# A graph network on one core: source rows of the first stage gathered during the dense pass and kept in a table in DRAM

## What is computed

```
def _gin_conv(x, src, dst, wa, ba, wb, bb):
    agg = segment_sum(x[src], dst, num_segments=N_NODES)
    h = x + agg
    h = relu(h @ wa + ba)
    return h @ wb + bb
```

## Time and profile before

| | |
|---|---|
| median of 3 runs | 4950.94 us (4936.32 to 4970.49) |
| the profiled execution, by its own time | 4992.41 us |
| its span, first to last instruction | 4990.6 us |
| mean granted TensorE clock | 0.735 of full |
| POOL busy | 1923.9 us (39%), 1994 instructions |
| PE busy | 3052.7 us (61%) |

### The profile page before, as it was taken

The page is one execution under the profiler, slowest core; times in us unless marked ns, Lnnn a source line. Parts: engine busy times, 40 slices in busy tenths (PEclk is TensorE's granted clock), DMA queues, the critical chain, the costliest instruction groups (busy, mean ns, idle before and its releaser), DMA issues. The chain is left out here.

```text
span 4990.6 us, 67455 instructions
## 1 busy us (share of the span) xinstructions
PE 3052.7 (61%) x18081; PEld 2462.8 (49%) x18081; DVE 2653.8 (53%) x8166; ACT 2245.8 (45%) x5893; POOL 1923.9 (39%) x1994
## 2 busy tenths in 40 slices
PE   1182019997887787785663059991089891068665
PEld 1062007775443454443563049890089891067664
DVE  2092009998343655896562017770047881078875
ACT  0082008885111344674552027770056770066765
POOL 6606750000554554663664720007700007700455
PEclk8596559998776878997786569885588875576655
DMA  3292016665554343454663237672256762255443
GB/s 115 68 341 101 12 38 221 221 224 171 139 153 118 95 108 109 135 170 136 185 202 106 63 114 232 203 220 65 59 182 203 221 198 80 65 173 193 137 130 93
DMA packets 419338, 723.50 MB, mean 145 GB/s; under 512 B 76431, under 2 KB 137908, under 8 KB 418606
## 3 DMA queue, kind: packets, MB, share of 16 engines
q1 hardware_dynamic: 350990, 610.53, 37.8%
q0 software_dynamic: 63040, 107.35, 8.6%
q10 hardware_dynamic: 5024, 2.30, 0.2%
HBM read 428.65 MB, written 321.10 MB: 150 GB/s over the span
## 5 line engine op out<-in xcount | busy, mean ns | idle before, releaser
L683 POOL DMA_INDIRECT msgs<-t_gat,row_i x591 | 567.1, 960 | 1180.2 <-DMA t_gat<-t_hn 951.1
L1738 PE MATMUL t_p_q<-mean_col,t_nsq 128*128 128x1 f32 x2352 | 344.5, 268 | 285.7 <-issue 228.5
L1738 PEld LDWEIGHTS t_p_q<-mean_col,t_nsq 128*128 128x128 f32 x2352 | 354.5, 231 | 297.3 <-issue 297.3
L2246 ACT ACTIVATE t_nnt<-t_p_nt,cxt 128x512 f32<-128x512 f32 x294 | 200.6, 682 | 614.3 <-remote 235.6
L699 POOL DMA_INDIRECT dg_g_ring<-t_xw,src_i x197 | 189.6, 962 | 669.1 <-DVE slot_id L1202 603.6
L2083 PE MATMUL t_p_nt<-ident,t_nh 128*128 128x128 f32 x1176 | 222.6, 322 | 252.2 <-issue 181.0
L1731 PE MATMUL t_p_nh<-wx,t_nnt 128*128 128x132 f32 x1568 | 261.0, 317 | 188.0 <-issue 138.6
L2006 POOL DMA_INDIRECT out_rows<-t_hn,own_i x197 | 200.5, 1018 | 416.8 <-issue 336.6
L1731 PEld LDWEIGHTS t_p_nh<-wx,t_nnt 128*128 128x128 f32 x1568 | 224.7, 218 | 189.0 <-issue 188.9
L2083 PEld LDWEIGHTS t_p_nt<-ident,t_nh 128*128 128x128 f32 x1176 | 163.2, 166 | 267.9 <-issue 252.5
L1752 DVE TENSOR_TENSOR t_hn<-t_p_nh,t_ninv 128x264 f32<-128x264 f32 x392 | 151.4, 428 | 257.8 <-remote 194.2
(11 more groups left out here) (410 smaller groups left out, 8730.8 us busy)
## 6 DMA issues: line engine op xcount, KB each, us to landing
t_gat<-t_hn SPq DMA_DIRECT2D x296, 264.0 KB
t_nh<-t_gat SPq DMA_DIRECT2D x294, 264.0 KB
t_x<-de_x SPq DMA_DIRECT2D x196, 256.0 KB
t_ah<-t_gat SPq DMA_DIRECT2D x150, 264.0 KB
t_gat<-de_h SPq DMA_DIRECT2D x98, 264.0 KB
t_xw<-in_x_map SPq DMA_DIRECT2D x28, 903.0 KB
de_xt<-in_x_t SPq DMA_DIRECT2D x98, 256.0 KB
t_xn<-t_x SPq DMA_DIRECT2D x98, 256.0 KB
```

Source lines behind the costliest of these rows:

```text
L683: self.nc.gpsimd.indirect_dma_start(out=self.msgs[:, c, 0:width], out_offset=None, in_=table, in_offset=bass.IndirectOffsetOnAxis(ap=idx[: ...
L1738: last = self.nc.tensor.matmul(p_q[:, j:j + 1], sq[:, j * D:(j + 1) * D], self.mean_col[:], start=True, stop=True)
L2246: nc.scalar.activation(nnt[:, g % 2], p_nt[:], ACT.Identity, bias=bias).then_inc(act_nt, 1)
```

## The change

POOL no longer fills the ring for gin1 directly. During the dense pass it gathers each group of source rows into the same ring, waits until the group before has landed, and writes that group with a plain DMA of its own to a new table in DRAM, `t_xs` (128 x 200 x 129 numbers). The place in the ring is free again when the write of four groups earlier has landed (`kept`). In gin1 SP loads each group from the table into a new tile `xs` of four groups, ahead of the flags; it waits for the group's write, and for PE and DVE to have left the tile's place. PE and DVE wait for this load where they waited for the gathers. SP's steps of gin1 are written out, where they were a loop.

```
-        def rows(i):
-            u = i % UN
-            if i >= UN:
-                pool.wait_ge(turned, i - UN + 1)
-                pool.wait_ge(taken, i - UN + 1)
-            for j in self.filled(i):
-                nc.gpsimd.indirect_dma_start(
-                    out=ring[:, u, j, :], out_offset=None, in_=self.xw,
-                    in_offset=bass.IndirectOffsetOnAxis(ap=self.src_i[:, i * G4 + j:i * G4 + j + 1], axis=0)).then_inc(arrived[u], 16)
...
-        for i in range(AG):
-            rows(i)
+        for i in range(AG + 1):
+            if i < AG:
+                u, c0 = i % UN, i * G4
+                if i >= UN:
+                    pool.wait_ge(kept[u], 16 * (i // UN))
+                for j in self.filled(i):
+                    nc.gpsimd.indirect_dma_start(
+                        out=ring[:, u, j, :], out_offset=None, in_=self.xw,
+                        in_offset=bass.IndirectOffsetOnAxis(ap=self.src_i[:, c0 + j:c0 + j + 1], axis=0)).then_inc(arrived[u], 16)
+            if i > 0:
+                u, c0, n = (i - 1) % UN, (i - 1) * G4, len(self.filled(i - 1))
+                pool.wait_ge(arrived[u], self.ring_rows((i - 1) // UN + 1, i - 1))
+                nc.gpsimd.dma_start(self.xs[:, c0:c0 + n, :], ring[:, u, 0:n, :]).then_inc(kept[u], 16)
...
+            xs = sb("xs", [128, UN, G4, MW])
+            arrived = [sem(f"arrived{u}") for u in range(UN)]
...
                     if live(k, u, 0, AG):
+                        c0, n = i * G4, len(self.filled(i))
+                        sp.wait_ge(kept[u], 16 * (i // UN + 1))
+                        wait(sp, s["pe_t"], i - UN + 1)
+                        wait(sp, s["dve_row"], i - UN + 1)
+                        sp.dma_start(xs[:, u, 0:n, :], self.xs[:, c0:c0 + n, :]).then_inc(arrived[u], 16)
                         wait(sp, s["dve_s"], i - UN + 1)
...
-                steps(sp, AG, 6, step, 2)
+                written_out(AG, 6, step)
...
-                        pe.wait_ge(arrived[v], self.ring_rows(k + (0 if u < 1 else 1), i - 1))
+                        pe.wait_ge(arrived[v], 16 * (k + (0 if u < 1 else 1)))
```

More of the change, by code:

```diff
@@ L245, in allocate @@
         self.xw = xw[0:NPAD * MW].rearrange("(r w) -> r w", w=MW)
+        self.xs = nc.dram_tensor("t_xs", (128, CHUNKS, MW), F32, kind="Internal").ap()
         self.unplaced = xw[NPAD * MW:NPAD * MW + SLOTS].rearrange("(p c) -> p c", p=128)
@@ L685, in resident_gather, with slot_gathers @@
                 in_offset=bass.IndirectOffsetOnAxis(ap=idx[:, c:c + 1], axis=0), **bound).then_inc(arrived, 16)
-    def slot_gathers(self, pool, ring, sem, arrived, turned, taken):
+    def slot_gathers(self, pool, ring, sem, arrived, kept):
         nc, a = self.nc, self.a
         mapped = sem("g_mapped")
-        def rows(i):
-            u = i % UN
-            if i >= UN:
-                pool.wait_ge(turned, i - UN + 1)
-                pool.wait_ge(taken, i - UN + 1)
-            for j in self.filled(i):
-                nc.gpsimd.indirect_dma_start(
-                    out=ring[:, u, j, :], out_offset=None, in_=self.xw,
-                    in_offset=bass.IndirectOffsetOnAxis(ap=self.src_i[:, i * G4 + j:i * G4 + j + 1], axis=0)).then_inc(arrived[u], 16)
         self.resident_gather(self.dst_i, a["x"], D, self.got, range(FIRST, FIRST + EVERY * COPIES))
@@ L1048, in hidden, with gin1_part @@
         return t[:, bass.ds(g, 1), 0:GN].rearrange("p o f -> p (o f)")
-    def gin1_part(self, block, sem, xs, arrived, turned, taken):
+    def gin1_part(self, block, sem, kept):
         nc, a = self.nc, self.a
@@ L1065, in gin1_part @@
             names = ("pe_x", "pe_r", "pe_a", "pe_b", "pe_h", "dve_b", "act_a", "act_b", "dve_s", "dve_r", "dve_e",
-                     "dve_h", "least", "mix", "blank_rows")
+                     "dve_h", "least", "mix", "blank_rows", "pe_t", "dve_row")
             s = {n: sem(n) for n in names}
-            s["pe_t"], s["dve_row"] = turned, taken
             own = lambda c: self.msgs[:, bass.ds(c, 1), 0:D].rearrange("p o f -> p (o f)")
@@ L1200, in step @@
                     if live(k, u, 1, AG):
-                        dve.wait_ge(arrived[v], self.ring_rows(k + (0 if u < 1 else 1), i - 1))
+                        dve.wait_ge(arrived[v], 16 * (k + (0 if u < 1 else 1)))
                         nc.vector.tensor_copy(self.slot_id[:, bass.ds((i - 1) * G4, G4)], xs[:, v, :, D]).then_inc(s["dve_row"], 1)
@@ L1231, in phase_dense_gin1 @@
             arrived = [sem(f"g_arrived{u}") for u in range(UN)]
-            turned, taken = sem("g1_turned"), sem("g1_taken")
-            self.dense_part(block, lambda n: sem("de_" + n), lambda pool: self.slot_gathers(pool, ring, sem, arrived, turned, taken))
-            self.gin1_part(block, lambda n: sem("g1_" + n), ring, arrived, turned, taken)
+            kept = [sem(f"g_kept{u}") for u in range(UN)]
+            self.dense_part(block, lambda n: sem("de_" + n), lambda pool: self.slot_gathers(pool, ring, sem, arrived, kept))
+            self.gin1_part(block, lambda n: sem("g1_" + n), kept)
     def phase_gin2(self):
```

## The result

| | before | changed |
|---|---|---|
| median of 4 runs each | 4954.82 us (4936.32 to 4970.49) | 5054.97 us (5050.42 to 5075.88) |
| ratio of the two | | 1.0209, 95% interval 1.0178 to 1.0240 |
| span of the profiled execution | 4990.6 us | 5057.6 us |
| first scan of gin1 | 1233.8 us | 1459.4 us, +225.6 |
| first to last scan | 337.4 us | 221.3 us, -116.1 |

The change costs 100 us, 2.1%. Its sign, its place and its two opposite parts are as predicted. The loss in the dense pass is 48 us smaller than predicted.

What follows compares the result with a forecast made beforehand. The prediction took the phase up to gin1 as bound by POOL's issuing and PE, one after the other. Dense pass +274 and gin1 -112 gave +162 us, 4950.9 + 162 = 5113 us, range 4980 to 5190.

Steps and rivals of the forecast that it cites:

- its two opposite parts: Dense pass loses 274 us under POOL's added issuing; gin1 without POOL gains 112 us; together +162 us.
- The main step: Dense pass: POOL's unbroken issuing lasts 289 us longer, delaying PE's signals; gin1 then runs at 4.54 us a step.
- Rival A: Dense pass: lag doesn't follow the gathers, which stay hidden; only gin1's gain is left, 4839 us; chance 0.09.
- The rule quoted from the Trainium skill: Engines: only DVE and GpSimd share a port, PE and ACT never wait; by it the 274 us would be nearly nothing.
- the 62 predicted for the writes: POOL in the dense pass: 50 table writes, each priced at a gather's 1.25 us, 62 us in all.
- The new waits: POOL in the dense pass: waits for `arrived` and `kept` should be met when reached, costing nothing.
- The dense pass: Under 289 us more issuing at 123.2 us a group, 2.3 groups worth 15 us get done: loss 274 us.
- the 26 us of tail: Dense pass: lag outlasting POOL's last gather, 718.4 to 744.6 us, expected alike before and after the change.
- rival B: Dense pass: new waits open pauses letting others catch up; 4986 us; 0.15 including what lies between it and the forecast.
- C: POOL's writes are dear, 2.1 us each or more: 5156 us, or 5212 with late gin1 loads; 0.10 beyond the forecast's range.
- gin1: All 49 steps at 4.54 instead of 6.89 us: 115 us less, taken as 112 for the first steps' clock.
- the likeliest case: Whole kernel: forecast of 5113 us with its own range, 5060 to 5160 us, chance 0.66.

Runs made afterwards that it cites:

- paced kernels: Kernel before with POOL's dense-pass DMAs in bursts of five gathers or four scatters: 4576.39 us; changed kernel in bursts of five at most: ratios 0.992 and 0.9241.

## Why the prediction was right, and where it was off

**The main step held.** The gathers moved into the dense pass lengthen the time in which PE's signals come late; gin1 then has its undisturbed pace. Rival A, that they are hidden, gave 4839 us; the kernels with plain loads or no gathers came to 4836 and 4852 us, so its sum was near and only its condition wasn't met where the lag is. The rule quoted from the Trainium skill (page "SBUF — State Buffer", section "Who interferes with whom") can't be carried over to ACT's waits at semaphores: with the lag they were 44 to 48 us. On the chip without it the traces agree with the rule: PE does 1028 matmuls beside 120 DMAs of POOL.

**POOL's issuing.** Predicted to end at 1007 us, ended at 1000. From the first ring gather to the end it took 302.9 us, of which 197 gathers at 1.25 us are 246. The other 57 us stand against the 62 predicted for the writes, but that nearness is partly luck. A write with nothing else in the way adds 0.60 us, 30 us for 50, half the price chosen. The rest are 2.1 us of waits and some 25 us in which gathers and writes took longer than their median; by what, the trace doesn't tell, and without writes the gathers took longer still (1.39 us each). The new waits cost POOL next to nothing, as predicted (`kept` never, `arrived` those 2.1 us in 2 waits at the end).

**The dense pass.** Predicted +274 us, measured +225.6. The step that failed is that 123.2 us a group holds as long as POOL issues (289 / 123.2 = 2.3 groups), with the 26 us of tail behind it as before. The store of the same group is the place to compare: the one behind 677.54 in the earlier trace rows and the one behind 669.74 in the changed kernel, 793.01 us. SP's timeline of the kernel before has it here, when POOL had stopped:

```profile
749.62 0.36 SPq L804 DMA_DIRECT2D t_h<-de_h  x1
...
756.34 0.35 SPq L804 DMA_DIRECT2D t_h<-de_h  x1
```

From 793.01 to 1003.71 us four more groups passed, where the prediction's 123.2 us gives 1.7. By that count 0.6 + 4 = 4.6 groups were done from 718 to 1004 us, not 2.3, which is worth another 2.3 x 6.55 = 15 us, and the tail was 1003.7 - 1000.0 = about 4 us, not 26: another 22. With POOL's end 7 us earlier that makes 44 of the 48 us. The kernel without writes shows what did it: there the pace stays at 123 us a group. So the writes did it, as far as one run of that kernel shows. That they act as short pauses among the gathers, or by making the gathers rarer, fits the paced kernels, but neither was shown apart. It is rival B in a mild form, by the writes themselves and not by waits. Of C nothing came: the writes were not dear, and they eased the lag.

**gin1.** Predicted -112, measured -116.1 us (-103 on the third chip). 4.55 us a step. SP's loads are hidden but for 8.5 us at two waits.

**The stages behind.** Predicted unchanged. The phase gives +109.5 us, the start of the next stage's gathers likewise (1588.4 to 1697.9 us), the medians differ by 100. The next stage was 18 us shorter in the profiled run of the changed kernel (362.8 after 380.7 us, from its first gather to the next stage's), and 20 us longer on the third chip (397.5 after 377.1). So it varies between executions or chips, and not with the change. The two comparisons differ by 140 - 100 = 40 us, and 28 of them lie in the phase itself (+137.5 against +109.5 us): the lag eased less on the third chip, and gin1 gained less.

**Sum.** Forecast 5113, measured 5055 us: inside the range of 4980 to 5190, 5 us below the likeliest case's own range of 5060 to 5160. Of the predicted difference of 162 us 62 didn't come: 48.4 in the dense pass, 4.1 in gin1 and 9.4 behind the phase. Slower by over 1%, as 0.80 of the chance had it.

## What to carry to other kernels

Before work is moved "under" another stage, look at what that stage does while the engine that gets the work is issuing: here the time of a dense group with POOL busy and with POOL silent gave the sign of the change, and its cost in the dense pass within about a fifth (274 for 226 us). If indirect DMAs slow the other engines, pace them: a wait on the other engines' own progress after each four or five of them gained 7.4% where moving the gathers lost 2.1%. Whether four or five is the right number on a chip with the lag, and whether the pauses or the lower rate do it, is not shown. And measure on more than one chip: the change lost 2.1 and 2.7% in two comparisons with the lag, and on a chip without it its paced form gained 0.8%.

## What the runs showed of the hardware

- On two chips, indirect DMAs issued by POOL without a pause (one per 1.25 us) go with signals from PE on which ACT acts some 46 us after the matmul's end, and a dense group then takes 123 us instead of 6.55. Signals to PE aren't late: PE began 0.15 us behind DVE's step. On a third chip the same instructions leave no such mark: 1028 matmuls in 161 us instead of 42. What differs between the chips (or the times at which they were used), and by what way the signals are held up, stays open; no run here tells it.
- Plain DMAs from POOL (0.54 us, 116 in 100 us) don't do it, nor do memsets.
- With pauses of 1.8 us after every four indirect DMAs, and the lower rate that comes with them, the lag is lifted nearly whole: 1762 matmuls in 285 us, against 98 with the lag and 1924 on the chip without it. With 2.4 us after every four it is lifted for the most part, 523 matmuls in 100 us, after a delay of 100 us in which it had built up. A plain write after every four lifts it in part (62 and 92 matmuls in 100 us).
- A plain DMA of 128 rows of 2 KB costs POOL 0.58 us busy and, behind a gather, adds 0.60 us to its stream, less than a gather of 128 rows of 516 bytes with its 0.95 and 1.25 us.
- PE's granted clock was 0.51 to 0.57, at or near the 1.2 GHz level, wherever the signals were late and PE mostly idle, and 0.99 to 1.00, the 2.4 GHz level, once the dense pass ran at its full pace. The lag costs PE its clock as well, but that is the small part: L843 takes 1.06 us there and 0.59 us at the full clock, beside waits of 44 to 48 us.
